# Group norm on VectorE: chunk 0's variance ahead of chunk 1's statistics, and the normalised tiles shared out 3 + 5

## The reference, cut to what matters

```python
def _gn(v, G=32, eps=1e-05):            # v is (16, 16, 16, 256)
    g = v.reshape(B_, H_, W_, G, C_ // G)
    m = jnp.mean(g, axis=(1, 2, 4), keepdims=True)
    s = jnp.var(g, axis=(1, 2, 4), keepdims=True)
    return ((g - m) / jnp.sqrt(s + eps)).reshape(v.shape)

x = x + _L0_conv_ref(_gn(x), t, weights1, ke_weights, ke_bias)   # 16 Fourier modes along 256 channels
t = _to_tokens(x)
t = t + _L1_attn_ref(_ln_t(t), W_q, W_k, W_v, W_o)               # causal attention, 256 tokens in each of 16 sequences
t = t + _L1_ffn_ref(_ln_t(t), router_w, w_fc, w_proj)            # 8 experts, two for each token
```

## Time and profile before

| | |
|---|---|
| time of 3 runs, median (lowest to highest) | 649.36 us (648.44 to 649.78) |
| the profiled execution: time, span of its instructions | 649.04 us, 647.3 us |
| busy over the span: PE, DVE, ACT, POOL | 604.6, 484.2, 412.5, 384.0 us |
| mean granted TensorE clock | 0.992 |

### The profile page before, as it was taken

The page is one execution under the profiler, slowest core; times in us unless marked ns, Lnnn a source line. Parts: engine busy times, 40 slices in busy tenths (PEclk is TensorE's granted clock), DMA queues, the critical chain, the costliest instruction groups (busy, mean ns, idle before and its releaser), DMA issues. The chain is left out here.

```text
span 647.3 us, 15234 instructions
## 1 busy us (share of the span) xinstructions
PE 604.6 (93%) x4726; PEld 578.9 (89%) x4726; DVE 484.2 (75%) x1164; ACT 412.5 (64%) x729; POOL 384.0 (59%) x284
## 2 busy tenths in 40 slices
PE   1798999999988998989999999999999999999993
PEld 1697888888878998989999999999999999999993
DVE  7667668789878897677886777778768778776761
ACT  2814577766677776787756657667566566666661
POOL 6101111575767776456676676776676767777783
PEclk9999999999998999999999999999999999999997
DMA  8910011233688795753223132131231321312211
GB/s 348 310 34 2 17 48 36 75 125 112 209 285 331 223 243 139 246 153 60 35 48 51 33 58 41 33 66 33 44 55 33 58 41 33 59 26 43 35 27 16
DMA packets 37597, 62.48 MB, mean 97 GB/s; under 512 B 3696, under 2 KB 32944, under 8 KB 36400
## 3 DMA queue, kind: packets, MB, share of 16 engines
q1 hardware_dynamic: 16448, 36.19, 16.8%
q0 software_dynamic: 13296, 18.00, 15.3%
q10 hardware_dynamic: 7808, 7.74, 4.7%
HBM read 37.02 MB, written 24.89 MB: 96 GB/s over the span
## 5 line engine op out<-in xcount | busy, mean ns | idle before, releaser
L715 POOL TENSOR_TENSOR pj_lo<-w_ffn,pj_hi 128x1024 fp32r<-128x1024 f32 x66 | 161.3, 2451 | 84.9 <-ACT pj_hi L789 76.1
L1694 DVE TENSOR_TENSOR fc_lo<-w_ffn,fc_hi 128x1024 fp32r<-128x1024 f32 x78 | 109.2, 1437 | 52.4 <-ACT fc_hi L789 50.6
L704 POOL DMA_INDIRECT out<-y,add_id x71 | 112.3, 1582 | 42.4 <-issue 40.6
L789 ACT ACTIVATE pj_hi<-w_ffn 128x1024 fp32r x78 | 81.9, 1058 | 77.4 <-PE psO L2121 64.1
L2121 PE MATMUL psP<-pj_hi,h_hi 128*128 128x256 f32 x312 | 91.9, 295 | 5.1 <-DVE h_lo L1694 5.1
L789 ACT ACTIVATE fc_hi<-w_ffn 128x1024 fp32r x78 | 79.0, 1052 | 21.5 <-issue 20.3
L2121 PE MATMUL psP<-pj_lo,h_hi 128*128 128x256 f32 x312 | 87.9, 282 | 0.0
L2121 PE MATMUL psP<-pj_hi,h_lo 128*128 128x256 f32 x312 | 87.7, 281 | 0.0
L666 POOL DMA_INDIRECT slots<-rows,slot x64 | 68.8, 1075 | 22.0 <-issue 16.4
L656 POOL TENSOR_TENSOR roots<-ve,power 128x6 f32<-128x6 f32 (+2 forms) x20 | 23.1, 1154 | 83.8 <-DVE ve L1221 80.6
L2121 PE MATMUL psO<-pj_hi,h_hi 128*128 128x256 f32 x256 | 72.2, 282 | 0.0
(11 more groups left out here) (365 smaller groups left out, 1607.3 us busy)
## 6 DMA issues: line engine op xcount, KB each, us to landing
w_ffn<-in_w_ffn SPq DMA_DIRECT2D x8, 2048.0 KB, 9.2
xg<-slots ACTq DMA_DIRECT2D x25, 265.0 KB
xc<-in_x_ch SPq DMA_DIRECT2D x4, 1024.0 KB, 8.3
out<-x SPq DMA_DIRECT2D x16, 256.0 KB, 2.2
x<-in_x_tok SPq DMA_DIRECT2D x1, 3072.0 KB, 24.6
slots<-fill SPq DMA_DIRECT2D x9, 265.0 KB, 5.3
xg<-slots SPq DMA_DIRECT2D x7, 265.0 KB
out<-y,add_id POOLq DMA_INDIRECT x71, 4.0
```

The costliest lines, as they stand in the source:

```text
L704: nc.gpsimd.indirect_dma_start(out_d, bass.IndirectOffsetOnAxis(ap=add_id[:, s:s + 1], axis=0), y[:, s, :], None, compute_op=ALU.add).then ...
L715: nc.gpsimd.tensor_tensor(pj_lo[:, 4 * a:4 * a + 4, :], w_ffn[:, bass.ds(e, 1), (2 + a) * DFF:(3 + a) * DFF].rearrange("p a (c d) -> p (a ...
L789: nc.scalar.activation(out, src, ACT.Copy, **kw).then_inc(done, 1)
L1694: v.tensor_tensor(out, whole, upper.bitcast(F32), ALU.subtract).then_inc(done, 1)
```

## The change

- VectorE: `wabs_total` comes ahead of `time_weights`, which keeps only the two instructions that write `temb`. The two that square and add (`tsq`, `tpow`) become `time_powers`.
- VectorE: chunk 0's variance and scale come ahead of all statistics of chunk 1, with `time_powers` between the two. Chunk 1's eight statistics and its squares then follow in one piece, and the loop begins at chunk 2.
- ScalarE: the root `tabs` moves between the fourth and the fifth tile of chunk 0.
- The tiles are shared out anew. Before, ScalarE had all of chunk 2 and two tiles of chunk 3, and VectorE six of chunk 3. Now VectorE has the last three of chunk 2, between `norms_inverse` and the last variance, and the last five of chunk 3. ScalarE has five of chunk 2, and, behind the last root, three of chunk 3.

```diff
--- before.py
+++ after.py
@@ -401,7 +401,8 @@
 
             return (psS, psP)[c % 2]
 
-        GN_BY_DVE = 6
+        DVE_TILES = 3, 5
+        GN_BY_DVE = sum(DVE_TILES)
 
         def on(b):
 
@@ -755,8 +756,6 @@
             nc.scalar.activation(emb[:, :], ang[:, 0, :], ACT.Sin).then_inc(sin_ready, 1)
             act.wait_ge(wabs_step, 2)
             nc.scalar.activation(wabs[:, :], wsq[:, :], ACT.Sqrt).then_inc(wabs_ready, 1)
-            act.wait_ge(temb_step, 4)
-            nc.scalar.activation(tabs[:, :], tpow[:, :], ACT.Sqrt).then_inc(temb_ready, 1)
 
             def deviation(c):
 
@@ -772,15 +771,17 @@
                                          bias=gnb[:, c, n:n + 1]).then_inc(gn_done, 1)
 
             deviation(0)
-            normalised(0, range(CT))
+            normalised(0, range(4))
+            act.wait_ge(temb_step, 4)
+            nc.scalar.activation(tabs[:, :], tpow[:, :], ACT.Sqrt).then_inc(temb_ready, 1)
+            normalised(0, range(4, CT))
             deviation(1)
             normalised(1, range(6))
             deviation(2)
             normalised(1, range(6, CT))
-            normalised(2, range(5))
+            normalised(2, range(CT - DVE_TILES[0]))
             deviation(3)
-            normalised(2, range(5, CT))
-            normalised(3, range(CT - GN_BY_DVE))
+            normalised(3, range(CT - DVE_TILES[1]))
 
             act.wait_ge(temb_ready, 1)
             nc.scalar.activation(tpow[:, :], tabs[:, :], ACT.Exp, scale=-1.0).then_inc(exp_loaded, 1)
@@ -1085,6 +1086,9 @@
                 for c in range(2):
                     v.tensor_scalar(temb[:, c, :], psT1[:, c * HT:(c + 1) * HT], bias[:, c:c + 1], None,
                                     ALU.add).then_inc(temb_step, 1)
+
+            def time_powers():
+
                 dve.wait_ge(temb_step, 2)
                 v.tensor_tensor(tsq[:, :, :], temb[:, :, :], temb[:, :, :], ALU.mult).then_inc(temb_step, 1)
                 dve.wait_ge(temb_step, 3)
@@ -1132,10 +1136,23 @@
 
             wabs_squares()
             gn_statistics(0, range(CT))
+            def gn_normalised(c, tiles):
+
+                dve.wait_ge(gn_rs, c + 1)
+                for n in tiles:
+                    tile = gn_tile(c, n)
+                    v.tensor_scalar(tile, tile, grs[:, c, n:n + 1], gnb[:, c, n:n + 1], ALU.mult,
+                                    ALU.add).then_inc(gn_done_dve, 1)
+
             gn_squares(0)
+            wabs_total()
             time_weights()
-            wabs_total()
-            for c in range(1, CHUNKS):
+            gn_variance(0)
+            time_powers()
+            gn_scale(0)
+            gn_statistics(1, range(CT))
+            gn_squares(1)
+            for c in range(2, CHUNKS):
                 gn_statistics(c, range(4))
                 gn_variance(c - 1)
                 gn_statistics(c, range(4, 6))
@@ -1143,14 +1160,10 @@
                 gn_statistics(c, range(6, CT))
                 gn_squares(c)
             norms_inverse()
+            gn_normalised(CHUNKS - 2, range(CT - DVE_TILES[0], CT))
             gn_variance(CHUNKS - 1)
             gn_scale(CHUNKS - 1)
-
-            dve.wait_ge(gn_rs, CHUNKS)
-            for n in range(CT - GN_BY_DVE, CT):
-                tile = gn_tile(CHUNKS - 1, n)
-                v.tensor_scalar(tile, tile, grs[:, CHUNKS - 1, n:n + 1], gnb[:, CHUNKS - 1, n:n + 1], ALU.mult,
-                                ALU.add).then_inc(gn_done_dve, 1)
+            gn_normalised(CHUNKS - 1, range(CT - DVE_TILES[1], CT))
 
             dve.wait_ge(ld_attn, 16)
             v.tensor_copy(causal_16[:, :], causal).then_inc(mask_ready, 1)
```

## The result

Over 18 runs of each, the changed kernel takes 650.95 us (649.28 to 652.18) and the kernel before 649.52 us (648.44 to 650.48): ratio 1.002, interval 1.0012 to 1.0029, so 0.8 to 1.9 us slower. Forecast were 649.8 us and "no difference". The time lies 0.15 us outside the range. The means over the runs lie 1.3 and 0.7 us above those of the kernel before, 1.0 over both sets (0.6 to 1.3).

A forecast was written before the change was run, and what follows sets the result against it. The bound was taken to be the start of `spectra(1)`, behind a chain over VectorE's chunk work. The sum +0.81 - 0.34 = +0.47 us gave 649.51 against the profiled 649.04, or 649.8 as median; range 648.4 to 650.8.

The forecast's parts named there:

- the chain over VectorE: Group norm: the start of `spectra(1)` at 31.27 us hangs on a chain mostly over VectorE's chunk work.
- the 1.5 us of idle time: VectorE, before chunk 0's variance: idle from about 10.65 us for 1.5, making chunk 1's squares 1.44 late.
- the holds of `tsq` and `tpow`: VectorE, between chunk 0's variance and scale: GpSimd's instructions hold the two, which take 0.5 and 1.0 us.
- ScalarE's earlier start that doesn't help: ScalarE starts chunk 0 at 14.55 us, 0.5 earlier, but then waits for chunk 1's variance.
- the covered three tiles and `tabs`: VectorE's three chunk 2 tiles hide in a 1.80 us wait (uncovered 1.02); ScalarE's `tabs` hides too (uncovered 0.22).
- a sign of being wrong: The prediction called itself wrong if GpSimd doesn't hold `tpow`, among other signs.
- Some 0.6 comes back at this step: Chunk 1's scale: product takes 0.17 us, not 0.54, and the root no longer stands behind ScalarE's eight tiles.
- +0.81: Chunk 1's `gnb` comes at 20.82 us, not 20.01, and the loop to chunk 3's `gnb` shifts equally.
- 0.34: End of group norm: VectorE has five last tiles, not six, which takes 0.34 us off.
- no hold: Rival: `tsq` and `tpow` fall between GpSimd's instructions; -0.64 to -0.34, 648.7 to 649.0 us; chance 0.13.
- late load: Rival: a late instruction load on VectorE or ScalarE adds 1.2 us, giving 651.0; chance 0.11 with like stalls.
- Absorbed: Rival: the late start vanishes in TensorE's 2.95 us of gaps behind 48 us; 649.4 us; chance 0.10.

The follow-up runs named there:

- both sets: The changed kernel measured twice against the kernel before, the second time on another chip: 650.95 us, ratio 1.002, then 650.75 us, ratio 1.0011.
- front_changed: The changed kernel, cut off behind the products with the time weights, one store of `zr` ending it: 40.42 us (40.31 to 40.71).
- front_before: The kernel before, cut off behind the products with the time weights, one store of `zr` ending it: 39.61 us (39.49 to 40.65).
- the cut-off kernels: Kernels ended behind the time-weight products: new order with old tile sharing 40.81 us, changed kernel 40.38, quick runs of the kernel before 39.46 to 39.49.
- short_psum: The kernel before, cut off without the two fill stores, `gnb` reading the mean from PSUM: 39.39 and 39.58 us, and 40.54 to 40.98.
- the delay of 0.42: The kernel before with four idle copies on VectorE between the last scale and its six tiles: 649.42 us, ratio 1.0002.
- filled: The changed kernel with chunk 1's first four statistics in the wait and time powers ahead of chunk 1's variance: 648.82 us, 0.9991; again 648.98, 0.9990.
- tiles_only: The kernel before, VectorE's order kept, with only the new tile sharing (3 + 5): 650.09 us, ratio 1.0012.
- order_only: The changed kernel with tiles shared as before (all of chunk 2 on ScalarE, six of chunk 3 on VectorE): 649.89 us, ratio 1.0006.

## Why the prediction was wrong

**The reading of the kernel** was right: the chain over VectorE, the 1.5 us of idle time (1.58), the holds of `tsq` and `tpow` (0.53, 0.95), ScalarE's earlier start that doesn't help, the covered three tiles and `tabs`. In the execution profiled every mark lies within 0.1 us. In others the marks of `gnb` are met though the holds are not as forecast: in three of seven traces of the new order `tpow` isn't held (0.17 or 0.18), which the prediction named as a sign of being wrong, and what that saves is what the variance was late before it. That the marks fit there is luck.

**The step that failed** is a size: "Some 0.6 comes back at this step", the term that made chunk 1's `gnb` +0.81 late and not more. It set the new order, which is never held there in its full traces (in one cut off, `front_changed`, `gnb` took 0.34), against one execution of the old order that was. From the squares of chunk 1 to its `gnb` have 4.11 us, `front_before` 3.73, the changed kernel 3.51. So 0.2 comes back and not 0.6, and the old order's usual chain is 0.3 shorter at `zr` (32.14 against 32.47). In the traces chunk 1's `gnb` is ready at 19.64 in `front_before` and at 20.91 in the changed kernel, +1.27 where the sum had +0.81. By the cut-off kernels the order costs 1.3 where the sum had 0.81, and the tiles give 0.43 where it had 0.34: +0.9 and not +0.47, against executions of the old order that aren't held or late. The rival "no hold" thought of the hold on `tsq` and `tpow` in the new order; that GpSimd's hold in the old order might be the accident was not weighed, though the margin stood in the rows (VectorE at 19.47, GpSimd at 19.27). The run meant to take this hold away, `short_psum`, met none, so the cause rests on the traces and on the times of the cut-off kernels. The range failed with the sum: its upper end, 650.8, had no term behind it but a part of the late load, and the median came 0.15 above.

**Passing it on.** That a late start reaches the end fits the two numbers, 0.8 to 0.9 in group norm and 1.0 (0.6 to 1.3) at the end over 30 runs, but isn't shown: with two idle activations more, the same change came out at -0.1 us (-0.9 to +0.8), and the delay of 0.42 at 0.2. The first measurement's 1.3 in the mean, 1.4 in the median, leaves 0.4 to 0.5 over; scatter is the nearest explanation, as 0.9 lies in its interval of 0.8 to 1.9. The other comparison leans against a pure one to one: `filled` gains 1.35 and keeps 0.6 to 0.8 in the means, with 1.35 just inside both intervals. If something is lost, the nearest place is the issue at 265 us: in the six full traces with the tiles 3 + 5 it lasts 4.42 to 5.21 us, in the five without 1.44 to 4.44. But these are single traces and nothing was changed at that place, so it is argued and not shown.

**Open** stay: whether the tiles' 0.43 reaches the end (`tiles_only` and the difference from `order_only` to the changed kernel say no, each within twice its uncertainty), whether the two instructions that ScalarE has fewer play a part, and how often the full kernel before is held or late, which sets what the change costs in the median.

**The rivals.** "Absorbed" and "no hold" are out for the first measurement: the end is 0.8 to 1.9 us late, and `spectra(1)` is late in every trace of the change. No late instruction load was seen in group norm. The result lies on the border of 0.2% that the prediction drew between same and slower; it gave slower 0.13. The terms were known to 0.1 us in one execution, and I took that for the uncertainty of the median.

## What to carry to other kernels

When a sum is made against one profiled execution, look for the stalls in that execution that hang on a race, here a hold decided by under 0.1 us between two engines of which one waits for a transfer, and work the sum out with and without them. Ask the same of the new order: here a hold behind the late point made up for a late start. A piece of work moved ahead of its input's partner leaves a hole: before a variance is put first, see what fills the 2 us that TensorE's means take. And to measure a few tenths in the first 40 us of a 650 us kernel, cut the kernel off behind them: the scatter fell from 1 us to 0.1 to 0.2 within a group of runs. Look at the groups too: two orders that differ by 0.9 in quick executions differed by 0.1 over all.

## What the runs showed of the hardware

- A VectorE instruction with two SBUF inputs that starts 0.01 us behind a GpSimd instruction waits for all of it (0.73 us for 0.17 of work), and one that starts 0.07 us ahead of it isn't held. The Trainium skill's page "SBUF — State Buffer", section "Who interferes with whom", says that a VectorE instruction with two SBUF inputs contends with a GpSimd instruction that reads SBUF, and that issue order decides who blocks; the traces agree on VectorE's side (0.73 and 0.17). That GpSimd is blocked when VectorE is first doesn't show: its instruction took 0.72 us there and 0.71 in the other trace. With one input in PSUM, `gnb` took 0.17 in all four chunks of `filled`, and there chunk 0's ran from 13.47 in the middle of a GpSimd instruction (13.04 to 14.08). In `short_psum` it took 0.17 too, but none started under a GpSimd instruction.
- The first chunk's statistics started between 6.83 and 8.08 us in the traces, by the landing of a transfer issued at 1.7 us. The squares behind them took 0.18 to 1.08 us, by where they fell between GpSimd's instructions.
- ScalarE's issue of a 265 KB transfer during loads of 2 MB each took 1.44 to 5.21 us, against 0.34 to 0.40 for its other 31 issues in the traces.
- A stretch of 3.41 us at half the clock at about 202 us was in three of eleven full traces, two of the old order and one of the filled one. TensorE had waits of 0.5 to 1.0 us before it in the kernel before (194 to 202 us), and as long or longer ones in the changed kernel's trace, without the stretch.
